# A two-layer attention and feed-forward kernel: its gate stage split in halves, one inside the feed-forward's last turns, one inside the last stage

## What is computed

```python
x = x + xattn0(norm(x), ctx)            # 16 heads, softmax attention
x = x + ffn0(x)                         # two ternary matmuls, 256 -> 1024 -> 256, gelu and norms
q = norm(x); k = v = ctx                # layer 1: mLSTM-like attention, 8 heads
pre   = 15 * tanh((concat(q, k, v) @ ifgate_w.T + ifgate_b) / 15)
i_pre, f_pre = pre[..., :8], pre[..., 8:]
lf    = cumsum(log_sigmoid(f_pre))
log_d = lf[t] - lf[s] + i_pre[s]        # for s <= t, else -inf
m     = max(log_d over s)
d_mat = exp(log_d - m)
s_mat = (q @ k.T) / sqrt(32) * d_mat
x = x + rmsnorm(s_mat @ v / (max(|sum(s_mat)|, exp(-m)) + 5e-5)) * (1 + outnorm_w)
x = x + norm(x) @ weight.T + lora_experts(norm(x))   # softmax gate over 8 experts
```

## Time and profile before

| | us |
|---|---|
| median of 3 runs | 432.22 (431.83 to 432.54) |
| the profiled execution's own time | 433.9 |
| its span, first to last instruction | 432.0 |
| TensorE, VectorE, ScalarE, GpSimd busy | 344.1, 306.4, 248.9, 185.1 |
| mean granted TensorE clock | 0.916 of full |

### The profile page before, as it was taken

The page is one execution under the profiler, slowest core; times in us unless marked ns, Lnnn a source line. Parts: engine busy times, 40 slices in busy tenths (PEclk is TensorE's granted clock), DMA queues, the critical chain, the costliest instruction groups (busy, mean ns, idle before and its releaser), DMA issues.

```text
span 432.0 us, 9170 instructions
## 1 busy us (share of the span) xinstructions
PE 344.1 (80%) x3130; PEld 244.1 (57%) x3137; DVE 306.4 (71%) x1028; ACT 248.9 (58%) x470; POOL 185.1 (43%) x209
## 2 busy tenths in 40 slices
PE   2995698989999999824667776677489999999775
PEld 2774566767677777502445554355356666666422
DVE  3897454778898987676999999951537777787641
ACT  1564424664545545726788988874446666666520
POOL 2115200121212345149999999971004555445520
PEclk9999869999999999955999999989579999999965
DMA  7499999988476540000000000000001122212000
GB/s 242 136 281 281 273 303 289 242 167 150 95 148 112 127 71 2 1 0 0 2 1 2 0 2 1 2 0 2 0 14 27 37 51 50 50 39 39 24 25 24
DMA packets 48045, 35.78 MB, mean 83 GB/s; under 512 B 20096, under 2 KB 44032, under 8 KB 47872
## 3 DMA queue, kind: packets, MB, share of 16 engines
q1 hardware_dynamic: 48000, 35.20, 34.1%
HBM read 26.80 MB, written 8.39 MB: 81 GB/s over the span
## 4 chain that ended last, share of the span: by engine, by line
PE 53%; DVE 17%; issue 12%; ACT 5%; POOL 5%; DMA 3%; SPq 3%; DVEq 0%; POOLq 0%; ACTq 0%
PE PS L1438 6%; PE PS L1227 4%; PE PS L1216 4%; PE PS L1246 4%; DVE sm L736 4%; PE PS L1285 4%; PE PS L1428 4%; PE PS L1207 4%; PE PS L1206 4%; PE PS L1405 3%; DMA scr_k<-kpart 3%; PE PS L1423 2%; ACT pT L990 2%; SPq L315 2%; DVE sm L712 2%
## 5 line engine op out<-in xcount | busy, mean ns | idle before, releaser
L990 ACT ACTIVATE pT<-PS 128x512 f32<-128x512 f32 x64 | 36.6, 596 | 49.5 <-PE PS L1207 49.3
L605 DVE TENSOR_REDUCE negm<-PS 128x4 bf16<-128x512 f32 x64 | 42.4, 684 | 15.5 <-PE PS L1216 15.4
L434 POOL TENSOR_TENSOR sm<-sm,mhalf 128x1 f32<-128x1 f32 x16 | 11.3, 708 | 93.0 <-DVE sm L637 93.0
L450 POOL TENSOR_TENSOR kst<-kst,rows 128x1024 f32<-128x1024 f32 x16 | 37.6, 2351 | 5.0 <-ACT kst L1055 4.9
L464 POOL TENSOR_TENSOR kst<-kst,rows 128x1024 f32<-128x1024 f32 x16 | 37.8, 2365 | 0.0
L1320 PE MATMUL PS<-identf,w2f 128*128 128x128 f32 x128 | 19.2, 298 | 23.2 <-ACT w2f L1044 23.0
L1207 PE MATMUL PS<-identb,negm 128*128 128x128 bf16 x256 | 35.6, 222 | 0.0
L1227 PE MATMUL PS<-pT,vx 128*32 128x128 f32 x512 | 27.3, 287 | 5.0 <-ACT pT L990 5.0
L1320 PEld LDWEIGHTS PS<-identf,w2f 128*128 128x128 f32 x128 | 15.1, 151 | 27.7 <-ACT w2f L1044 22.4
L1438 PE MATMUL PS<-wd,xT 128*128 128x392 f32 x64 | 27.7, 560 | 1.8 <-DVE rest L884 1.8
L484 POOL TENSOR_TENSOR smd<-smd,mhalf 128x1 f32<-128x1 f32 x16 | 8.8, 550 | 44.9 <-DVE smd L915 44.9
(11 more groups left out here) (225 smaller groups left out, 1002.6 us busy)
## 6 DMA issues: line engine op xcount, KB each, us to landing
scr_q<-qpart SPq DMA_DIRECT2D x8, 384.0 KB, 4.9
scr_k<-kpart SPq DMA_DIRECT2D x8, 384.0 KB, 6.0
rows<-in_rows SPq DMA_DIRECT2D x1, 2056.0 KB, 11.3
X<-in_x SPq DMA_DIRECT2D x8, 256.0 KB, 4.7
CTXT<-in_ctxT SPq DMA_DIRECT2D x8, 256.0 KB, 4.6
cTb<-in_ctxT SPq DMA_DIRECT2D x16, 128.0 KB, 4.3
vx<-in_ctx SPq DMA_DIRECT2D x16, 128.0 KB, 2.7
out<-rest SPq DMA_DIRECT2D x16, 128.0 KB, 1.7
```

The costliest lines, as they stand in the source:

```text
L450: gp.tensor_tensor(n2[q.slot], n2[q.slot], ln2g, ALU.mult).then_inc(b_g2, 1)
L605: v.tensor_reduce(negm[f.slot % 2][:, 4 * hg:4 * hg + 4], PS[:, 2 + hg % 2, :].rearrange("p (h k) -> p h k", h=4), AX_X, ALU.max, negate=T ...
L990: s.activation(pT[:, hg, :], PS[:, hg % 2, :], ACT.Exp, scale=float(DH0) ** -0.5).then_inc(a_e, 1)
```

## The change

The gate stage is no longer a stage. Its 16 batches are done in two halves of 8 (`HB`), 64 columns each. Half 0 is spread over turns 16 to 19 of the feed-forward. Half 1 is spread over turns 4 to 8 of the last stage: transposes and bias in 4, capping and softplus in 5, sums and splitting in 6, placing in 7, the floors in 8. Turn 0 of the last stage (the gate argument of batch 0) stands on TensorE inside turn 19; turns 20 to 22 of the feed-forward stand in front of turns 1 to 3 of the last stage, on ScalarE behind turns 0 to 2.

The tanh is made of an exponential: `e2 = exp(2/15 pre)`, `th = 1 - 2/(e2 + 1)`, with two VectorE instructions and a reciprocal. Half 1's matmuls use bank 1, which is also the second half's of the gate argument and that of the expert layer's transposes, so TensorE waits in each of the turns 4, 6, 7 and 8, before the second half, until VectorE has read it. The feed-forward's gate product moves from bank 1 into bank 7 beside the `n3` transposes, the last three down products from bank 0 to bank 4, and in every feed-forward turn the down product now stands ahead of the `n3` transposes. GpSimd's and SyncE's programs stay as they are. A copy of `MPARTS` and `APARTS` becomes one cast (`AM`).

```diff
+            def biased(x, bank):
+                dve.wait_ge(g_tp, x + 1)
+                v.tensor_tensor(preg[:], PS[:, bank, 0:128].rearrange("p (b n) -> p b n", b=HB),
+                                gbias.unsqueeze(1).to_broadcast([128, HB, 2 * H1]), ALU.add).then_inc(g_pre, 1)
+
+            def capped(x):
+
+                dve.wait_ge(g_e2, x + 1)
+                link(v.tensor_scalar(e2[:], e2[:], 1e30, 1.0, ALU.min, ALU.add))
+                link(v.reciprocal(e2[:], e2[:]))
+                v.tensor_scalar(th[:], e2[:], -2.0, 1.0, ALU.mult, ALU.add).then_inc(g_th, 1)
+                dve.wait_ge(g_th, x + 1)
+                v.tensor_scalar(Ig[:], th[:, :, 0:H1], 15.0, None, ALU.mult)
+
...
+            def sums_copied(x, bank):
+                dve.wait_ge(g_sum, x + 1)
+                v.tensor_copy(Fs[:], PS[:, bank, 256:320])
+                v.tensor_copy(aT[:], PS[0:64, bank, 0:128]).then_inc(g_F, 1)
+                dve.wait_ge(g_F, x + 1)
+
...
+            def placed(x, bank):
+                dve.wait_ge(g_sel, x + 1)
+                v.tensor_copy(AM[:, :, 2 * x:2 * x + 2, :],
+                              PS[:, bank, :].rearrange("p (n q s) -> p n q s", n=2, q=2)).then_inc(g_A, 1)
+
+            def floor_argument(x, bank):
+                dve.wait_ge(g_mt, x + 1)
+                v.tensor_tensor(Mt[:], PS[:, bank, 0:64], Fs[:], ALU.subtract).then_inc(g_d, 1)
+
...
+                if tau == NB:
+                    biased(0, 4)
+                elif tau == NB + 1:
+                    capped(0)
+                elif tau == NB + 2:
+                    softplus_end(0)
+                elif tau == NB + 3:
+                    placed(0, 2)
+                    floor_argument(0, 3)
...
+                if tau == NB + 1:
+                    softplus(0)
+                elif tau == NB + 2:
+                    sums_copied(0, 3)
+                    gate_parts(0)
...
+                if t == 4:
+                    biased(1, 1)
+                elif t == 5:
+                    capped(1)
+                elif t == 6:
+                    softplus_end(1)
+                elif t == 7:
+                    placed(1, 1)
+                elif t == 8:
+                    floor_argument(1, 1)
                 if c:
...
+                if t == 6:
+                    sums_copied(1, 1)
...
+                if t == 5:
+                    softplus(1)
+                elif t == 6:
+                    gate_parts(1)
+
+            for t in range(1, NB + 5):
+                turn_cd(t, *peeled(t, NB, 4, 6))
...
+            def exp_of_pre(x):
+
+                act.wait_ge(g_pre, x + 1)
+                s.activation(e2[:], preg[:], ACT.Exp, scale=2.0 / 15.0).then_inc(g_e2, 1)
+
+            def exp_gate(x):
+                act.wait_ge(g_th, x + 1)
+                s.activation(eg[:], th[:, :, H1:2 * H1], ACT.Exp, scale=-15.0).then_inc(g_eg, 1)
+
+            def log_gate(x):
+                act.wait_ge(g_ug, x + 1)
+                s.activation(spg[:], ug[:], ACT.Ln).then_inc(g_ln, 1)
+
+            def floors(x):
+                act.wait_ge(g_d, x + 1)
+                s.activation(EM[:, x * HB:(x + 1) * HB, :].rearrange("p b h -> p (b h)"), Mt[:], ACT.Exp, scale=-1.0).then_inc(g_EM, 1)
...
+                if tau == NB + 1:
+                    exp_gate(0)
...
+                if tau == NB:
+                    exp_of_pre(0)
...
+                if tau == NB + 1:
+                    log_gate(0)
+                elif tau == NB + 2:
+
+                    s.activation(warm[:], mhalf[:, 0:1], ACT.Exp)
+                elif tau == NB + 3:
+                    floors(0)
 
             turn_a(*peeled(NB, NB, 4, 5))
...
+                if t == 5:
+                    exp_gate(1)
...
+                if t == 4:
+                    exp_of_pre(1)
+                elif t == 5:
+                    log_gate(1)
+                elif t == 8:
+                    floors(1)
+
+            for t in range(4):
+                turn_cd(t, *peeled(t, NB, 4, 6))
+                tau = NB + 4 + t
+                turn_b(tau, *peeled(tau, NB, 4, 9))
+            for t in range(4, NB + 5):
+                turn_cd(t, *peeled(t, NB, 4, 6))
 
 
         @block.tensor
...
+            def gate_columns(x, bank):
+                pe.wait_ge(b_PRE, HB * (x + 1))
+                for i in range(HB):
+                    at = (x * HB + i) * S
+                    last = t.transpose(PS[:, bank, i * 16:(i + 1) * 16], PRET[:, at:at + S], identf[0:16, 0:16])
+                last.then_inc(g_tp, 1)
+
...
+                if tau == NB:
+
+                    pe.wait_ge(b_hT, NB)
+                    gate_columns(0, 4)
...
                     if d.b == 0:
                         pe.wait_ge(s_tern, 2)
                         pe.wait_ge(a_e, 4 * NB)
                     pe.wait_ge(b_h2T, d.b + 1)
                     done(pe, b_x, d, 0)
+                    if d.b == NB - 3:
+                        pe.wait_ge(g_pre, 1)
+                    bank = 0 if d.b < NB - 3 else 4
                     for i in range(FC):
-                        last = t.matmul(PS[:, 0, 0:256], h2T[:, i, :], w2q[:, i, :], start=(i == 0), stop=(i == FC - 1))
+                        last = t.matmul(PS[:, bank, 0:256], h2T[:, i, :], w2q[:, i, :], start=(i == 0), stop=(i == FC - 1))
                     last.then_inc(b_m2, 1)
+                if f:
+                    if f.b == 0:
+                        pe.wait_ge(a_x, NB)
+                    pe.wait_ge(b_n3, f.b + 1)
+                    done(pe, b_PRE, f, 0)
+                    for i in range(KC):
+                        last = t.transpose(PS[:, 7, i * 128:(i + 1) * 128], n3[:, i * 128:(i + 1) * 128], identf[:])
+                    last.then_inc(b_t3, 1)
+                if tau == NB + 2:
+
+                    pe.wait_ge(b_hb, NB)
+                    gate_sums(0, 3)
+                elif tau == NB + 3:
+                    place_parts(0, 2)
+                    pe.wait_ge(g_F, 1)
+                    max_columns(0, 3)
+                    turn_cd(0, *peeled(0, NB, 4, 6))
                 if c:
                     if c.b == 0:
 
...
@@ -1418,6 +1514,15 @@
                     t.transpose(PS[:, 6, 0:128], gt[:], identf[:]).then_inc(d_gt, 1)
                 if n:
                     log_d(0)
+                if turn in (4, 7, 8):
+
+                    pe.wait_ge(d_xT, e.b + 1)
+                    if turn == 4:
+                        gate_columns(1, 1)
+                    elif turn == 7:
+                        place_parts(1, 1)
+                    else:
+                        max_columns(1, 1)
...
+                if turn == 6:
+                    pe.wait_ge(d_xT, e.b + 1)
+                    gate_sums(1, 1)
+
+                if turn == 4:
+                    pe.wait_ge(g_pre, 2)
+                elif turn == 6:
+                    pe.wait_ge(g_F, 2)
+                elif turn == 7:
+                    pe.wait_ge(g_A, 2)
+                elif turn == 8:
+                    pe.wait_ge(g_d, 2)
                 if n:
                     log_d(1)
...
 
-            pipeline(pe, NB, 4, 6, turn_cd)
+            turn_a(*peeled(NB, NB, 4, 3))
+            columns(Turn(1, 1, 0))
+            turn_a(*peeled(NB + 1, NB, 4, 3))
+            for tau in range(2, NB + 4):
+                turn_b(tau, *peeled(tau, NB, 4, 9))
+            for turn in range(1, NB + 5):
+                if turn < 4:
+                    tau = NB + 3 + turn
+                    turn_b(tau, *peeled(tau, NB, 4, 9))
+                turn_cd(turn, *peeled(turn, NB, 4, 6))
 
```

203 lines of the change are left out of this document (89 added, 114 removed).

## The result

The changed kernel takes **440.99 us** (median of 4 executions, 439.01 to 443.22) against 432.23 beside it: ratio 1.0203, 95% interval 1.017 to 1.0236. The forecast was 435.4 with a range of 428.5 to 440.0. The direction is right; the loss is 8.8 us where 3.2 was forecast, and the time lies 1 us above the range. Its profiled execution had a span of 439.0 and a time of 440.82, so 6.9 us over the profiled one of before, which itself stood 1.7 above its median.

A forecast was written before the change was run, and what follows sets the result against it. TensorE, busy 80% of the span, was taken to bound the kernel, fully in the last stage, with about 16 us open to cover. Terms -8.5 + 10.0 + 1.7 = +3.2 us gave 435.4 us, range 428.5 to 440.0.

The forecast's parts named there:

- Term 1: Gate work's first half in feed-forward turns 16 to 19: first scores at 302.2 in place of 316.59, gain 14.4 us.
- Term 2: Feed-forward turns 21 and 22 before last-stage turns 2 and 3: turns 1 and 2 grow to 7.8, gain shrinks to 8.5.
- Term 3: Gate work's second half in last-stage turns 4 to 8: delays adding up to 10.0 us, bounds 4.5 and 12.7.
- Term 4: TensorE's lower clock: 1.0 us for turn 6 and 0.7 for turns 19 and 20, 1.7 in all.
- rival (b): Half clock lasts in turns 19, 20 and 6: 438.7 us, or 440 with turn 7 too; chance 0.13.
- the signs: Right: scores about 302, turns 1, 2 at 7.8, turn 6 hole over 3 us; wrong: turns 5 to 7 under 23.
- Rival (d): Each ScalarE table switch takes 1.28 us more, two in turn 6 and two before: +5.1, 440.5 us; chance 0.03.
- Rival (a): Waits of turns 5 to 7 overlap, so the second half costs only 4.5 us: 428.2 us; chance 0.26.

The follow-up runs named there:

- e7: Changed kernel with the first half's exponentials and softplus differences in a PSUM bank, and one VectorE instruction in place of two: 435.81 us, ratio 1.0019 to before.
- e9: e7 with ScalarE copying the gate argument's columns (PRET) before the second exponential in turns 1 to 3 of the last stage: 433.24 us, ratio 0.9999 to before.
- e3: Changed kernel with 14 spare matmuls on TensorE in turn 6 before it waits for the gate product, nothing removed: 435.19 us, ratio 1.0048 to before.
- e15: e10 with 8 and 4 spare matmuls in feed-forward turns 17 and 18: 424.72 us, ratio 0.9788 to before.
- e10: e9 with the second half's steps spread over other places in turns 4 to 7, no work left out: 424.76 us, ratio 0.9824 to before.
- c1: The changed kernel itself measured once more, nothing altered: 439.86 us, ratio 1.0154 to before.
- e2: Changed kernel with the second half's logarithm replaced by a copy, so its two table loads go: 435.08 us, ratio 1.0013 to before.
- e13: e10 with the second half's logarithm back in its old place, ahead of turn 6's router exponential: 428.00 us, ratio 0.9885 to before.
- e12: Changed kernel with both the edits of e3 and e7 together: 434.36 us, ratio 0.9983 to before.

## Why the prediction was wrong in size

**Term 1** (first scores 302.2, gain 14.4): measured 304.50, gain 12.1. What failed is the list of what stands in front of batch 13's copy and batch 15's reduce. I added ScalarE's 3.4 us and priced VectorE's splitting steps by their rows in the gate stage, which held (2.13 us from 293.15 to 295.28, beside no pass, where 2.16 stood). But VectorE's capping and softplus steps of turn 17 stand at nothing in the sum. They are small in the gate stage, where GpSimd is idle, and were moved to turns where GpSimd works for nine tenths of the time. There they waited for its passes. With PSUM operands (e7) the stretch is 1.6 us shorter at nearly the same clock; the rest of what is missing goes with the clock in turns 17 and 18. The Trainium skill states the wait, page "SBUF — State Buffer", section "SBUF: two separate sides": VectorE in a two-port mode, or with two SBUF inputs against a GpSimd instruction that reads SBUF, and GpSimd take one port pair in turn, and whoever starts first holds it for its whole instruction. The rows agree, 2.21 and 2.27 us until a pass ends in place of 0.23 and 0.20.

**Term 2** (turns 1 and 2 at 7.8): measured 7.45 and 7.46. The mechanism, the transposes waiting for a copy behind the second exponential, is shown by e9, 0.85 us a turn. The scores of turn 4 were 6.9 us early, not 8.5.

**Term 3** (10.0 us): right. At whole clock (e3) turns 4 to 8 are 38.8 us in place of 29.4 before, 9.4. Its first large step, the router's exponential 5.5 us late, came out at 4.9: it starts at 340.50, where before's would stand at 342.44 - 6.87 = 335.57. Seven of the ten splitting steps cost 1.3, where ten were put at 2.1.

**Term 4** (half clock, 1.7; of it 1.0 in turn 6): here the prediction failed. In turns 6 and 7 it cost 1.6 + 3.1 = 4.7 us, where 1.0 stood, and before the first scores about 2 more (e15 against e10), partly in term 1 already and in turns 17 and 18, not 19 and 20. It was priced as an aftermath of the gap in turn 6 alone. But at half clock TensorE is busy for 3.00 of 3 us in both turns, so its slower matmuls are hidden by nothing, and turn 7 dropped again behind a wait of only 1.67 us, which in e3 dropped nothing. The bound of 2.5 us for turn 6 was just reached in c1; that turn 7 could pay more than that again was only in rival (b), which had turn 7 at half clock at 440 and got 0.13.

Put together, from the forecast +3.2: term 1 short by 2.3, turns 1 and 2 better by 0.7, term 3 better by 0.6, the half clock of turns 6 and 7 4.7 where 1.0 stood, less the 0.7 for turns 19 and 20, which ran whole. That is +7.2; measured between the profiles +6.9 to 7.1. By how little the time left the range says nothing: the second measure of the same kernel, 439.86, lies inside it. The step that failed is term 4, by 3.7 us.

Against **the signs**: first scores (304.50), turns 1 and 2 (7.46) and turn 4 (6.9 earlier) come near what was named; the hole over 3 us behind two loads is there (3.46), as is 5.90 from turn 9 on; turns 5 to 7 together are 31.0 us, far over the 23 below which I would have been wrong. Rival (d), the drained switch, is out: at 337.64 to 340.50 two loads and a logarithm follow each other without idle time, and e2 prices both loads at 2.19. Rival (a), the gain stays, needed the exponential close behind nd. It is 3.5 us behind (337.02 to 340.50). e10 shows that the 4.6 us for turns 4 to 8, rival (a)'s 4.5, could be had by another order.

## What to carry to other kernels

Work moved under another stage has to be priced with that stage's neighbours: look who shares a port with the engine, and take the duration from a row where both are busy. A stall of the matrix engine can cost twice, once as a wait and again as slower matmuls behind it (turn 6 of the changed kernel; not turn 6 of e13, where it waited 2.68 us); a kernel of the same code with spare matmuls in the gap tells the two apart. Before a difference between two profiles is put down to an edit, compare the clock of the stretch in both. A table switch is cheap where its engine waits anyway; here the same two loads cost 1.6 us more in one place than in another.

## What was not expected of the hardware

- VectorE's steps of 0.20 to 0.23 us (SBUF to SBUF, or two SBUF operands) took up to 2.27 us beside a GpSimd pass of 2.35; with one operand or the output in PSUM they took 0.23 to 0.28, and a one-operand reduce of 1.22 us lost nothing.
- Fourteen matmuls that compute nothing made the kernel 5.8 us faster (440.99 to 435.19; by the ratios of the two measures of the changed kernel, 6.7 and 4.6).
- The same wait of 1.67 us in turn 7 came before a fall of the clock to 0.50 in the changed kernel and before none in e3. What decides that is not settled by these runs.
- Code that is the same almost up to there reached turn 16's down product anywhere from 271.4 to 275.0 us in twelve profiles of the changed kernel and its variants, e12's throttled one left out (before 272.51), so an instant of the second half of a trace says less than a distance from a mark near it.
